# Relative attention with experts: reads of the relative keys put behind the next write, relative values in eight portions, expert weights fetched one by one

## What is computed

```python
qkv = layernorm(x) @ w_attn                     # q, k, v: (8, 16, 512, 8)
rel = tril(idx[:, None] - idx[None, :])         # distance t - s
rk, rv = embk[rel], embv[rel]
att = einsum('bhtd,bhsd->bhts', q, k) * scale + einsum('bhtd,tsd->bhts', q, rk)
att = softmax(where(causal, att, -inf))
y = einsum('bhts,bhsd->bhtd', att, v) + einsum('bhts,tsd->bhtd', att, rv)
x = x + y @ w_proj
x = x + experts(layernorm(x))
```

## Time and profile before

| | |
|---|---|
| median of 3 runs | 851.3 us (845.1 to 855.38) |
| profiled execution | 854.7 us |
| its span, first to last instruction | 853.0 us |
| share of the span busy | PE 84%, DVE 70%, ACT 60%, POOL 30% |
| mean granted clock of PE | 0.946 of full speed |

### The profile page before, as it was taken

How to read it: one execution, slowest core, us unless ns; L and a number is a source line. 1 busy time by engine, 2 the same in 40 slices (tenths; PEclk the granted TensorE clock), 3 DMA queues, 4 the chain that set the end, 5 groups by cost and what they waited for, 6 DMA issues and landing times. The chain is left out here.

```text
span 853.0 us, 27128 instructions
## 1 busy us (share of the span) xinstructions
PE 717.1 (84%) x10368; PEld 522.4 (61%) x10368; DVE 594.8 (70%) x2036; ACT 512.4 (60%) x1031; POOL 255.2 (30%) x253
## 2 busy tenths in 40 slices
PE   3667569898597888877989777988799999999998
PEld 2345447676465766655768565767666666666665
DVE  6835458878477696767778657867746767766776
ACT  2565478687486685877768667758733434534331
POOL 8333236433235442435534333543300000000000
PEclk9877799999999898999999999989979999999999
DMA  9789989677788667569767658864200000000000
GB/s 312 235 277 286 351 259 273 183 211 207 233 244 241 188 181 215 169 202 290 220 170 217 180 159 250 259 190 128 74 2 20 25 26 25 13 13 13 13 13 13
DMA packets 116687, 140.32 MB, mean 164 GB/s; under 512 B 8848, under 2 KB 83088, under 8 KB 116368
## 3 DMA queue, kind: packets, MB, share of 16 engines
q1 hardware_dynamic: 116560, 138.59, 53.9%
HBM read 82.26 MB, written 56.30 MB: 162 GB/s over the span
## 5 line engine op out<-in xcount | busy, mean ns | idle before, releaser
L979 DVE CUSTOM_DVE_ANT_0 ps<-ps,near 128x128 f32<-128x128 f32 (+3 forms) x512 | 241.6, 510 | 146.3 <-PE ps L759 77.0
L906 ACT ACTIVATE work<-ps,nmin 128x128 f32<-128x128 f32 (+3 forms) x512 | 246.3, 539 | 112.7 <-DVE nmin L979 107.0
L771 PE MATMUL ps<-ident,work 128*128 128x128 f32 x1280 | 213.1, 288 | 20.8 <-issue 19.9
L771 PEld LDWEIGHTS ps<-ident,work 128*128 128x128 f32 x1280 | 158.7, 147 | 55.9 <-issue 34.7
L759 PE MATMUL ps<-kb,qb 128*128 128x128 bf16 (+3 forms) x512 | 134.2, 315 | 42.6 <-ACT work L906 36.3
L720 POOL TENSOR_SCALAR_AFFINE_SELECT work<-work 128x512 f32<-128x512 f32 x96 | 60.9, 635 | 299.9 <-ACT work L895 297.3
L1298 ACT ACTIVATE near<-ps 128x512 f32<-128x512 f32 x80 | 47.6, 595 | 137.1 <-PE ps L1263 137.0
L724 POOL TENSOR_TENSOR work<-work 128x512 f32<-128x512 f32 x96 | 124.0, 1292 | 8.0
L964 DVE COPY work<-ps 128x512 f32<-128x512 f32 (+1 forms) x192 | 122.8, 639 | 5.2 <-PE ps L771 4.2
L788 PE MATMUL ps<-work,vb 128*9 128x128 f32 x2560 | 101.4, 287 | 4.0 <-ACT relS L884 2.5
L1273 PEld LDWEIGHTS ps<-work,near 128*128 128x128 f32 x640 | 82.6, 192 | 34.3 <-issue 31.7
(11 more groups left out here) (101 smaller groups left out, 653.3 us busy)
## 6 DMA issues: line engine op xcount, KB each, us to landing
near<-w_slots SPq DMA_DIRECT2D x96, 512.0 KB, 4.4
w_slots<-relS SPq DMA_DIRECT2D x128, 256.0 KB, 4.9
qk_rows<-work SPq DMA_DIRECT2D x48, 256.0 KB, 5.3
near<-w_slots SPq DMA_DIRECT2D x32, 256.0 KB, 5.0
w_slots<-near SPq DMA_DIRECT2D x8, 512.0 KB, 6.2
qb<-qk_rows SPq DMA_DIRECT2D x24, 96.0 KB
kb<-qk_rows SPq DMA_DIRECT2D x24, 96.0 KB
qb<-qk_rows SPq DMA_DIRECT2D x48, 48.0 KB
```

The costliest lines, as they stand in the source:

```text
L771: ins = nc.tensor.transpose(tp_ps[:, m % 2, n * P:(n + 1) * P], prob[:, m % PROBS, n * P:(n + 1) * P], ident[:, :])
L906: ins = nc.scalar.activation(prob[:, m % PROBS, h * wide:(h + 1) * wide], qk_ps[:, m % 3, h * wide:(h + 1) * wide], ACT.Exp, bias=nmin[:, ...
L979: nc.vector.tensor_tensor_reduce(out=scores, in0=scores, in1=near[:, q % NEAR, a, 4 * P - wide:4 * P, r], scale=1.0, scalar=3e38, op0=ALU. ...
```

## The change

Four things are altered. In the blocks 2 and 3, from the second stage on, the product of the relative keys is made 14 slots ahead of its quad in place of 10. In the blocks 2 and 3, the opening stage included, the read of the relative keys comes 5 slots after the product in place of 3; as products there are 4 slots apart, the order on SP becomes write q+1, read q, write q+2, read q+1. The relative values are multiplied in eight portions of half the size: the second half of an old portion comes half a quad later, so that the last one of a stage is issued up to two slots later, and the turning, the projection and the store after it with it; in block 0 both halves stay in one slot. The five loads of the experts' weights go out one by one, each in the first slot of one of the first five quads of group 1's block 1, in place of all at once in the block 2 ahead of it.

```diff
+WEIGHTS = 5
...
-        ahead = 8 if row(q) <= 1 else 10
+        ahead = 8 if row(q) <= 1 else 10 if q < QUADS else 14
...
-RVN = 4
+RVN = 8
...
 def rv_slot(e, c):
-    return last(QUADS * (e + 1) + (3 if row(QUADS * (e + 1)) == 0 else 1) + c) + AV_LAG
+    i = row(QUADS * (e + 1))
+    half = 4 // HEADS_OF[i] // 2
+    return last(QUADS * (e + 1) + (3 if i == 0 else 1) + c // 2) + AV_LAG + c % 2 * half
...
-READ_AT = [max(REL_AT[q] + 3, FIRST[max(q - NEAR + 1, 0)]) if REL_AT[q] else 0 for q in range(NQ)]
+READ_AT = [max(REL_AT[q] + (3 if row(q) <= 1 else 5), FIRST[max(q - NEAR + 1, 0)]) if REL_AT[q] else 0
+           for q in range(NQ)]
...
                             elif q == NI * QUADS:
                                 first["wait_rows"](sp)
-                                experts["weights"](sp)
                             load_v(q // QUADS // NI + 1)
+                    for k in range(WEIGHTS):
+                        if m == FIRST[QUADS * (NI + 2) + k]:
+                            experts["weights"](sp, k)
...
-    def load_weights(sp):
-        for dst, src in ((gw, gate_w), (gb, gate_bias), (w1_sb, w1), (w3_sb, w3), (w2_sb, w2)):
-            sp.dma_start(dst, src).then_inc(w_in, 16)
+    def load_weights(sp, k):
+        dst, src = ((gw, gate_w), (gb, gate_bias), (w1_sb, w1), (w3_sb, w3), (w2_sb, w2))[k]
+        sp.dma_start(dst, src).then_inc(w_in, 16)
```

## The result

The changed kernel takes 807.21 us in the median of four runs (804.24 to 809.5), the kernel before beside it 852.41. The ratio is 0.948, with a 95% interval from 0.941 to 0.955. The profiled execution takes 809.15 us (span 807.4) at a mean granted clock of 0.962, against 854.7 at 0.946.

What follows compares the result with a forecast made beforehand. SP's serial queue of writes and reads, not an engine, was taken to pace the attention. Terms -19 - 2 - 3 - 1 + 1 + 2 = -22 on 852 gave 830 us, range 814 to 845.

Steps and rivals of the forecast that it cites:

- What bounds the kernel: Attention: SP's in-order loop of write, landing and read, not an engine, sets 5.26 us a quad; experts stay at 241 us.
- Block 2: Three block-2 stages, groups 1 to 3: PE decides at 95%, 4.24 us a quad; -10.0, -4.5, -4.5, together -19 (-14 to -23).
- Block 0: Stages of block 0 in groups 1 to 3: product of keys not moved, no gain booked, 0.
- Block 3 and the portions: Block 3, four stages: -2 (0 to -8) from SP's loop; eight portions outside block 0: -1 (bound -16 to +0).
- risk of +2: PE's and DVE's gaps, hidden so far by waits for keys, come out in the three stages: +2, 0 to +9.
- Opening stage: Start of the kernel, near what transfers allow, only the order changes: -3, from -7 to +5.
- Weights: Loads issued one by one in block 1 of group 1, mostly hidden by the reads' lead: +1, 0 to +6.
- The -7.3 booked inside block 2: Group 1's block 2: the quad behind the weights' burst gains -6.3, the next one at lower clock -1.0.
- Block 1: Block 1 was given only the cost of the weights' loads moved there: +1, 0 to +6.
- More is won: Rival: block 2 -23, block 3 -8, opening stage -5, portions -4; 815 us; for it DVE's 68.0 us for products; chance 0.09.
- PE runs out of instructions more often: Rival, PE's queue in blocks 1 to 3: each further gap costs 4.6 us, seven make it slower, 860 us; chance 0.06.
- PE falls to its lower level: Rival, blocks 2: short portions with gaps drop PE's clock, 24 quads at 5.0 us, +18, 848 us; chance 0.04.

Runs made afterwards that it cites:

- output steps kept: The changed kernel with its eight portions, but turning, normalised form and projection in the slots they had with four portions: 819.97 us, 0.964 to before.
- four moved portions: The changed kernel with four whole portions in place of eight, each moved half a quad on, output steps following at the same distance: 807.25 us, 0.950 to before.
- only the output steps later: The changed kernel with four whole portions in their old slots and just the output steps one or two slots later: 821.25 us, 0.965 to before.

## Why the prediction was right or wrong

**What bounds the kernel: right.** The loop of SP set 5.26 us a quad, the experts stayed at 241 us, and the order is worth 27 us alone and 33.5 on top of the other parts. SP's wait for landed writes fell under 60 us as forecast (49.4), its wait for copies grew (143.9), and DVE's wait for keys fell under 5 (3.1).

**Block 2: the mechanism right, the size low** (-25.0 against -19). The prediction applied its 95% of PE's busy time to four quads of a stage and then took "-4.5 again at the least" for group 3, which gave 9.7. The 11.4 us of idle PE in that stage were in the row that the prediction quoted and were not used. Applied to the whole stages of the groups 2, 3 and 1, PE's 33.94, 33.06 and 35.72 us give 35.7, 34.8 and 37.6; measured are 37.3, 34.8 and 36.0. The two sums are the same, 108.1, and that is in part luck, for PE is busy for 88, 94 and 92% of these stages. Plain quads mostly take 3.1 to 3.9 us, not 4.24; the last ones, which carry keys and output steps, take 5.4 to 6.7.

**Block 0: missed** (-8.7 against 0). Its own reads were not moved, and so it was left at nothing. But SP entered block 0 late with its writes, as late as the loop of block 2 had made it, and a stage of 16 us has no room to recover. DVE's wait for keys in these stages, 8.6 us before and 0.3 after, is the term that was put at nothing. In the table the kernels with the read moved have 38.7 to 43.5 us there (49.7 with the output steps kept), those without 46.0 to 49.6. A stage behind a late queue belongs to the sum.

**Block 3 and the portions: the term that failed most** (-14.5 against -2 and -1). This is the step that failed. Without the portions the change stands at 0.964, that is 821.6 on 852.4 us, inside the forecast's range; eight portions on the opened order take off a further 13 to 24 us (0.948 and 0.936), where -1 was booked. Two things were wrong. First, block 3 was sized by what SP's loop leaves over PE's need (0.5 us a quad), and the portions by their own duration: "halves keep the sum", with PE's busy time as the price. But PE's *idle* time was what the portions change. The gaps that the prediction named in the earlier trace rows it took as a risk of +2 and as a rival that makes the kernel slower; they are in fact a cost of the old portions, 8.3 us of gaps in block 3 with stretches at half clock behind some of them. The bound of -8 was too near as well: it counted the 0.5 us in sixteen quads, and four stages hold thirty-two. Second, the two terms were added, and block 3 needs both parts: it takes 174.4 us before, 171.9 with the portions alone, 168.0 with the order alone, 174.2 with order and weights, and 159.9 and 161.2 with all. The gaps go with the portions; by what way the order helps there is open.

**Opening stage: right** (-3.3 against -3, 48.5 us, share 0.97 for 0.94). It goes with the place of the read: 47.8 to 49.2 us in the kernels that have it moved, 51.2 to 54.0 in the others.

**Weights: half right.** The burst went out of block 2 and no wait for keys came up in block 1, as forecast. But alone they moved the time by nothing, and on top of the rest by some 4.5 us, which is not settled. The -7.3 booked inside block 2 came for the larger part in the trace of the weights alone (48.0 to 43.5), but the time of that kernel did not fall.

**Block 1: worse than forecast** (+4.9 against +1). No wait for keys is the cause: DVE has none there. PE's gaps rose from 14.9 to 21.2 us. Kernels of the table with the lead of 14 slots have 128.0 to 139.7 us there and those with the lead of 10 have 118.9 to 127.9. In the change itself the lead of 14 costs block 1 6.4 us against the lead of 10 and brings 5.0 in block 3 and 3.4 in block 2.

**The rivals.** "More is won", at 815, came nearest. It had block 2, block 3 and the portions larger than the forecast, and still too small, but the reason it gave did not come: DVE's wait for products of scores is 76.5 us where it was 68.0. "PE runs out of instructions more often" fell as to the time: gaps of PE from 0.5 us on sum to 27.5 us after, 37.0 before. "PE falls to its lower level" fell too: the half-clock time from 118 us to the end of the attention fell from 41.0 to 13.3 us. The rule of the Trainium skill (Perfetto Trace Analysis, Matmul Optimizations) that matmuls should run back to back in batches did not decide here: on the opened order eight portions beat four in time and in granted clock (0.962 against 0.947 in the profiled executions), and two were slower than four. Sixteen lost again, so the runs show no rule the other way either.

**What stays open.** That placing the portions half a quad on takes most of the gaps out of block 3 is shown by the four moved portions (2.6 us, against 6.2 with only the output steps later). Why it does is not. Neither the meeting with the products of the values nor the length of a portion sorts the kernels by itself, since halves that meet them and whole portions that do not both leave few gaps. The row of small matmuls that PE gets at once sorts them in block 3, but not in block 2. In block 1 the gaps differ from kernel to kernel between 8.9 and 23.8 us with no rule found. Where the instructions lie in memory differs in all these kernels and could not be held fixed. None of the experiments beat the changed kernel by more than its interval.

## What to carry to other kernels

On a queue that issues in order, a read that waits for the landing of its own write holds back the next write: put the read behind the next write, and count what the queue's lateness costs the stages behind as well. Price a change of small matmuls by PE's idle time around them and by the clock behind the gaps, not by their busy time. When a stage has two causes of delay, removing one may show little; before sizing a stage, take each engine's busy time in the whole stage as the floor and ask which waits stand between.

## What the runs showed of the hardware

- **A gap of PE without a releaser often goes with an instruction fetch.** All nine such gaps of at least 1.5 us in the changed kernel end 2.3 to 2.6 us after a 16 KB packet of the instruction queue starts; in the change without portions all six do, in the kernel before four of seven. Over all eighteen traces it is 93 of 121, with the packet 2.25 to 2.7 us ahead of the end, and of the gaps from 0.5 to 1.5 us about half (116 of 238). 84 packets run in every kernel, and most of them go with no gap. This fits the statement of the Trainium skill (Runtime: NRT & Kernel Launch, Instruction fetch mechanics) that crossing a block of instructions is mostly hidden. Where it is not, a gap that goes with one lasts up to 3.5 us here (in the change without portions). That the fetch causes the gap is argued from the times, not shown.
- **A gap can cost twice.** After 3.21 us of idle PE the granted clock fell to the 1.2 GHz level and four turnings took 1.06 us in place of 0.60. Block 3 without a long gap takes 40.2 us, with 3.8 us of gaps 45.9 and 46.5 where the clock fell, and with 3.8 and 3.3 us of them 43.6 where it did not.
- **Transfers changed their landing when the order changed.** The issues of the whole run answer to the earlier trace rows:

```profile
near<-w_slots SPq DMA_DIRECT2D x96, 512.0 KB, 5.4
w_slots<-relS SPq DMA_DIRECT2D x128, 256.0 KB, 4.3
```

Reads land in 5.4 us in place of 4.4 and writes in 4.3 in place of 4.9. The reads, each issued behind the next write now, take a microsecond longer. No price of it is seen, as DVE waits for keys for 3.1 us in all.
